# One decoder layer on one core: projections and self-attention in one stage, with the last batch's projections inside the first attention slots

## The reference, cut to what matters

```
y = _layernorm(x, ln1_w, ln1_b)
qkv = (y @ w_qkv).reshape(b, n, 3, H, DK)
attn = softmax(einsum('bhnd,bhmd->bhnm', q, k) / sqrt(DK))
y = einsum('bhnm,bhmd->bhnd', attn, v) ... @ w_proj
x = x + y
```

## Time and profile before

| | us |
|---|---|
| median of 3 runs (lowest, highest) | 1640.35 (1637.45, 1640.81) |
| the profiled execution | 1641.96 |
| its span, first to last instruction | 1640.2 |
| PE busy | 1514.0 (92%) |
| DVE busy | 1118.4 (68%) |
| ACT busy | 870.0 (53%) |
| POOL busy | 378.9 (23%) |
| stage project_qkv, first transpose to last copy of v | 390.6 to 504.6 |
| stage self_attention, first score to last exponential | 513.9 to 1239 |

### The profile page before, as it was taken

How to read it: one execution, slowest core, us unless ns; L and a number is a source line. 1 busy time by engine, 2 the same in 40 slices (tenths; PEclk the granted TensorE clock), 3 DMA queues, 4 the chain that set the end, 5 groups by cost and what they waited for, 6 DMA issues and landing times. The chain is left out here.

```text
span 1640.2 us, 44928 instructions
## 1 busy us (share of the span) xinstructions
PE 1514.0 (92%) x18412; PEld 1078.9 (66%) x18412; DVE 1118.4 (68%) x1679; ACT 870.0 (53%) x1577; POOL 378.9 (23%) x601
## 2 busy tenths in 40 slices
PE   6999699986886999999999999999998939999997
PEld 3555366653542666666666766666666839999997
DVE  4546398886645898889889888988974753333332
ACT  1222465654441788888888888888885301111111
POOL 4110222222431111111111111111110113454453
PEclk9999799999996999999999999999999859999999
DMA  7000000000322111111111111111103935655652
GB/s 227 1 0 20 20 2 2 1 2 20 131 87 103 36 37 39 42 38 37 42 39 37 39 40 38 38 40 38 38 21 105 311 108 195 212 191 198 212 190 81
DMA packets 80330, 125.38 MB, mean 76 GB/s; under 512 B 22243, under 2 KB 46437, under 8 KB 80134
## 3 DMA queue, kind: packets, MB, share of 16 engines
q1 hardware_dynamic: 74518, 107.24, 21.0%
q0 software_dynamic: 5616, 15.34, 2.6%
HBM read 96.03 MB, written 26.08 MB: 74 GB/s over the span
## 5 line engine op out<-in xcount | busy, mean ns | idle before, releaser
L1287 DVE TENSOR_REDUCE sb_m_mx<-banks 128x1 f32<-128x1024 f32 x512 | 603.3, 1220 | 70.6 <-PE banks L1155 62.9
L1253 ACT ACTIVATE sb_m_pT<-banks 128x512 f32<-128x512 f32 x1024 | 556.6, 595 | 117.7 <-PE banks L1182 106.6
L1182 PE MATMUL banks<-sb_m_q,sb_m_k 99*32 99x512 bf16 x4096 | 467.6, 381 | 0.9 <-ACT sb_m_pT L1253 0.5
L1155 PE MATMUL banks<-sb_m_k,sb_m_q 96*32 96x512 bf16 x4096 | 368.0, 388 | 12.9 <-DMA sb_m_k<-k_parts 10.5
L1197 PE MATMUL banks<-sb_m_pT,sb_m_v 128*32 128x256 f32 x4096 | 314.5, 378 | 0.7 <-ACT sb_m_pT L1253 0.7
L1182 PEld LDWEIGHTS banks<-sb_m_q,sb_m_k 99*32 99x32 bf16 x4096 | 179.1, 96 | 79.2 <-ACT sb_m_pT L1253 6.0
L1155 PEld LDWEIGHTS banks<-sb_m_k,sb_m_q 96*32 96x32 bf16 x4096 | 160.3, 96 | 93.0 <-DVE sb_m_mx L1287 20.1
L1197 PEld LDWEIGHTS banks<-sb_m_pT,sb_m_v 128*32 128x32 f32 x4096 | 177.4, 109 | 58.0 <-ACT sb_m_pT L1253 1.2
L1800 ACT ACTIVATE sb_e_hT<-banks 128x512 f32<-128x512 f32 x78 | 46.6, 597 | 237.9 <-PE banks L1760 237.9
L1125 POOL CAST sb_m_mx_parts<-sb_m_mxT 8x128 bf16<-8x128 f32 x64 | 18.1, 283 | 592.4 <-issue 564.4
L1760 PEld LDWEIGHTS banks<-sb_e_xT,w 128*128 128x128 f32 x1248 | 148.1, 195 | 4.3 <-DVE sb_e_xT L1810 2.4
(11 more groups left out here) (216 smaller groups left out, 1876.4 us busy)
## 6 DMA issues: line engine op xcount, KB each, us to landing
w<-in_w SPq DMA_DIRECT2D x47, 1024.0 KB, 5.2
sb_m_q<-q_parts SPq DMA_DIRECT2D x384, 32.0 KB, 1.8
sb_m_k<-k_parts SPq DMA_DIRECT2D x384, 32.0 KB, 1.8
q_parts<-sb_c_parts SPq DMA_DIRECT2D x24, 256.0 KB, 2.2
k_parts<-sb_c_parts SPq DMA_DIRECT2D x24, 256.0 KB, 2.3
X<-in_x SPq DMA_DIRECT2D x4, 1024.0 KB, 10.7
x_rows<-X SPq DMA_DIRECT2D x8, 512.0 KB, 9.5
z_rows<-sb_g_zs SPq DMA_DIRECT2D x8, 512.0 KB, 5.1
```

Of the source, the lines that this page charges most:

```text
L1155: mm = pe.matmul(ps[2 * (k % 2) + h][c:c + 32, :], q_s[0:R, i, k * P + c:k * P + c + 32], k_s[0:R, i, h * 512:(h + 1) * 512], start=True, ...
L1182: mm = pe.matmul(ps[rotating(use)][c:c + 32, :], k_s[:, i2, m * P + c:m * P + c + 32], q_s[:, i2, h * 512:(h + 1) * 512], start=True, stop ...
L1253: act.activation(pT[:, m, h * 512:(h + 1) * 512], ps[rotating(f"b{m}{h}")][:, :], ACT.Exp).then_inc(exped, 1)
L1287: dve.tensor_reduce(mx[:, par % 2, k:k + 1], pz[:, 2 * (k % 2):2 * (k % 2) + 2, :].rearrange("p q n -> p (q n)"), AX.X, ALU.max).then_inc( ...
```

## The change

project_qkv and self_attention give way to one stage, project_and_attend, with one block. The instructions of the attention's slots are those of before, line for line, but for what is shown here. What moves:

- **The last batch.** Batches 0 to 2 are projected ahead as before. The four units of batch 3 stand in slot 0, a half before each "a", and its v in slot 1, a tile before each "a". VectorE's four remainders of batch 3 stand in slot 0 behind the tops 0, 2, 4 and 6. The maxima turned in slot 1 take bank 7, and the last banks of v are 4, 5, 6 and 5.
- **The order in batches 0 to 2.** xT is double (xT_mem and vblk_mem). TensorE transposes the next batch before it makes v of this one; ScalarE copies those tiles out around the last middle. VectorE's order is: both halves and norm of r = 0, first_half of r = 1, remainder 0, second_half, remainder 1, norm, remainder 2, remainder 3. GpSimd makes both powers ahead of the batch's four lows.
- **The fill of rows 96 to 98 of k_s** comes behind remainder 3 of batch 2 on VectorE; TensorE waits for it before slot 0.
- **SyncE** loads head 0 behind the stores of batch 1 and head 1 behind those of batch 2, stores the units of batch 3, and then goes on with slot 1: the load of head 2, the maxima of head 0, and so on.
- **Memory.** xs_c and one xT lie in the upper half of y_all, the other xT and the remainders in vblk_mem and kblk_mem. All loops over batches are written out.

```
 SyncE
+            for b in range(B):
+                for u in range(U):
+                    store(b, u)
+                if b == 1:
+                    batch_stored(0)
+                    load(0, 0)
+                if b == 2:
+                    load(1, 1)
...
-                if has(s, -1, edge):
+                if s > 0 and has(s, -1, edge):
+                    if (s + 1) % H == 0:
+                        batch_stored((s + 1) // H)
 GpSimd
+            for b in range(B):
+                if b < B - 1:
+                    scale(b, 0)
+                    scale(b, 1)
+                for u in range(U):
+                    pool.wait_ge(mid_done, U * b + u + 1)
+                    need(pool, stored[u % 2], 48 * (U // 2 * b + u // 2))
+                    pool.tensor_tensor(parts[:, u % 2, 2, :], rest[:, u % 2, :], parts[:, u % 2, 1, :],
+                                       ALU.subtract).then_inc(low_done, 1)
...
+                    if (s - 2) % H == 0:
+                        pool.wait_ge(v_copied, v_ready((s - 2) // H))
 TensorE
+            turn_tiles(0)
+            for b in range(B - 1):
+                for u in range(U):
+                    unit(b, u, 0)
+                    unit(b, u, 1)
+                turn_tiles(b + 1)
+                for i in range(TPB):
+                    values(b, i)
+
+            pe.wait_ge(set_up, 3)
...
+                if s == 0:
+                    unit(B - 1, 0, 0)
+                    for k in range(TPB):
+                        if k < TPB - 1:
+                            unit(B - 1, (k + 1) // 2, (k + 1) % 2)
+                        a(k)
+                    return
+                if s == 1:
+                    for k in range(TPB):
+                        values(B - 1, k)
+                        a(k)
+                        if k == 2:
+                            maxima()
+                    return
 ScalarE
+            take_tiles(0, 0)
+            take_tiles(0, 1)
+            for b in range(B):
+                for u in range(U):
+                    if u >= 1:
+                        middle(b, u - 1)
+                    high(b, u)
+                if b < B - 1:
+                    take_tiles(b + 1, 0)
+                middle(b, U - 1)
+                if b < B - 1:
+                    take_tiles(b + 1, 1)
+                    for u in range(2):
+                        act.wait_ge(v_done, 2 * b + u + 1)
+                        take_values(b, 4 + 2 * u, 4 * u, 2)
 VectorE
+            for b in range(B - 1):
+                first_half(b, 0)
+                second_half(b, 0)
+                norm(b, 0)
+                first_half(b, 1)
+                remainder(b, 0)
+                second_half(b, 1)
+                remainder(b, 1)
+                norm(b, 1)
+                remainder(b, 2)
+                remainder(b, 3)
+                if b == B - 2:
+                    dve.memset(k_s[R:R + 3, :, :], -1.0).then_inc(set_up, 1)
...
+                for k in range(4):
+                    top(k)
+                    if s == 0 and k in (0, 2):
+                        remainder(B - 1, k // 2)
...
+                for k in range(4, TPB):
+                    top(k)
+                    if s == 0 and k in (4, 6):
+                        remainder(B - 1, k // 2)
 decoder
-                    tensors(ahead, [("w_qkv", [P, KT, 3 * D], F32), ("ln1_w", [P, KT], F32), ("ln1_b", [P, KT], F32),
-                                    ("xs_c", [P, TPB, D], F32)])
+                    tensors(ahead, [("w_qkv", [P, KT, 3 * D], F32), ("ln1_w", [P, KT], F32), ("ln1_b", [P, KT], F32)])
+                    half = t["y_all"][:, B * H // 2:, :, :].rearrange("p h n d -> p (h n d)")
+                    t["xs_c"] = half[:, 0:TPB * D].rearrange("p (n d) -> p n d", d=D)
+                    t["xT_mem"] = half[:, TPB * D:].rearrange("p (k n) -> p k n", k=KT)
                     t["qkv_in"] = ahead.enter_context(nc.semaphore("qkv_in"))
                     run(cross_attention)
-                    run(project_qkv)
-                run(self_attention)
+                    run(project_and_attend)
```

365 lines of the change are left out of this document (added).

## The result

| | before | after |
|---|---|---|
| median, lowest to highest, us | 1640.07 (1637.45 to 1640.81) | 1616.25 (1612.86 to 1618.15) |
| profiled execution, its span | 1641.96, 1640.2 | 1616.15, 1614.2 |
| first transposes of the stage to b(0, 0) | 143.4 | 117.7 |
| b(0, 0) to the start of the last exponential | 704.6 | 703.0 |

What follows compares the result with a forecast made beforehand. TensorE bounds the attention from slot 2, so only the stretch before shrinks: b(0, 0) from 533.94 to 509.5, 24.4 us, or 26.8 at full clock. Taking 25 from 1641.96 gives 1617.0, 1615.4 against the median; range 1608 to 1625.

Steps and rivals of the forecast that it cites:

- The frame: Attention from slot 2 on: bound by TensorE and left alone, so an earlier b(0, 0) is carried to the end.
- Batches 0 to 2: Projection ahead of slot 0: 26.8 us a batch in place of 29.1, remainder 3 of batch 2 ending at 471.2.
- the ring of 29.1: Old batches: transposes wait for the previous batch's v, that for remainder 3, that for the norm; 29.1 us a batch.
- Slot 0: Batch 3's units beside the "a": TensorE 8 x 2.2 = 17.6 us, to 492.4; remainder 3 ends at 495.2.
- Slot 1: Batch 3's v beside the "a": VectorE through at 506.0 after 10.8 us, TensorE a little before.
- SyncE's queue: End of slot 1: head 2's load and the maxima's DMAs stand behind the last store, putting b(0, 0) at 509.5.
- the new wait: TensorE at b(0, 0), for the maxima: some 3.5 us behind the work that was before it.
- The clock: Start of slot 2: half clock cost up to 2.4 us before; gain 26.8 at full clock, 24.4 if it falls again.
- The norm beside two lows: VectorE's norm r = 1 in batches 0 to 2: stretched from 15.8 to 22.1 by GpSimd's lows, at no cost.
- keep 29: Rival, batches 0 to 2: they keep 29.1 us, b(0, 0) comes 7 us later, time 1622; chance 0.12.
- both rivals of the half clock: TensorE at half clock in slots 0 and 1 (1637, or 1630 for slot 0 alone; 0.06), or already in batches (1694; 0.04).
- the slower one: Rival, batches 0 to 2: half clock where TensorE waits for remainders and stores, 45.8 us a batch, 1694; chance 0.04.

Runs made afterwards that it cites:

- e1: Changed kernel with batch 3 projected ahead of slot 0, so slots 0 and 1 hold only scores and maxima; 1623.22 us, ratio 0.9887.
- e9: Changed kernel with the old order on VectorE and GpSimd and one xT, only the one stage left; 1620.66 us.
- e5: Changed kernel with slots 0 and 1 in pairs: a whole unit or two tiles of v, then two "a"; 1615.67 us.
- e3: Changed kernel with head 2's load issued behind the second store of batch 3, not the fourth; 1611.50 us, ratio 0.9818.
- e4: Changed kernel with head 3's load too issued on SyncE before the DMAs of head 0's maxima; 1622.23 us.
- e6: Changed kernel with the fill moved to the head of VectorE's stream, ahead of the first bn_stats; 1620.84 us.
- e7: Changed kernel with GpSimd beginning a batch's lows only when the norm r = 1 is done; 1628.76 us.
- e2: Changed kernel with the old order of VectorE and GpSimd in batches 0 to 2, xT still double; 1629.44 us, ratio 0.9935.
- e8: Changed kernel with one xT, the next batch's transposes behind v again, VectorE's new order kept; 1626.98 us, ratio 0.9916.
- e11: Changed kernel with old order and double xT, plus five unused matmuls on TensorE ahead of each batch's transposes; 1621.06 us.

## Why the prediction was right, and where only its number was

**The frame held.** The steady slots are untouched (11.07 us each in both kernels), so what slot 2 gained stayed. But b(0, 0) at 509.73, where 509.5 was forecast, is partly luck: the stage began 1.5 us later. Counted from the first transposes, 118.9 was forecast and 117.7 measured.

**The number.** The stage gained 27.5 us in the profiles, near the 26.8 that the prediction had for full clock; it took 25. The median fell by 23.8, because 1.5 went to the later start and because the profiled execution of the kernel before lies 1.9 above its median. That 25 and 23.8 agree so well is luck too.

**Where the 25.7 came from.** The profiles of before, e1 and after cut at the start of remainder 3 of batch 2, and e9 beside them:

```profile
473.16 1.23 DVE L1001 SCALAR_TENSOR_TENSOR sb_c_rest<-banks,sb_c_parts 128x1024 f32<-128x1024 f32 x1 [0.19 <-DVE xs_c L988]
...
470.38 1.23 DVE L517 SCALAR_TENSOR_TENSOR kblk_mem<-banks,sb_m_parts 128x1024 f32<-128x1024 f32 x1 [2.03 <-ACT sb_m_parts L421]
...
468.90 1.22 DVE L520 SCALAR_TENSOR_TENSOR kblk_mem<-banks,sb_m_parts 128x1024 f32<-128x1024 f32 x1 [2.04 <-ACT sb_m_parts L424]
...
470.20 1.21 DVE L520 SCALAR_TENSOR_TENSOR kblk_mem<-banks,sb_m_parts 128x1024 f32<-128x1024 f32 x1
```

The first transposes lie at 390.58, 393.53, 392.05 and 393.18 in these profiles. So up to the cut it takes 82.6 before and 76.9 after, 5.7 us; from it to b(0, 0) 60.8 before, 46.9 in e1, 40.8 after. The 13.9 between before and e1 are the joint between the stages, with the meeting of the engines, the fill and the load of head 0, and in them some 2 that e9 gives to the transposes of batch 3 ahead of v: the joint alone is about 12. The last 6.1 are the overlap of batch 3. The prediction gave joint and overlap as one sum, 21; with those 2 they are 20. It had 3 for the batches up to the cut, where 5.7 came.

**"Batches 0 to 2" is the step that failed in its cause.** It forecast 26.8 a batch and it was 26.0, and the chain by which it was worked out is the one in the trace: the norm ends, then a high part that waited 3.9 for its store. But it gave as the reason that the double xT breaks the ring of 29.1. e9 has that ring whole, on the old order, and batches of 27.9, 27.0 and 27.0; at the cut it stands at 77.0, where the kernel before had 82.6. So nearly all of the 5.7 came neither from the double xT nor from the order. The kernel before ran at half clock for 3.4 us in its v of batches 0 and 1. The second half of v of batch 0, before and in e9:

```profile
415.73 5.41 PE L941 MATMUL banks<-w_qkv,sb_c_xT 128*128 128x256 f32 x16 [2.11 <-DVE sb_c_rest L1001]
...
417.48 3.72 PE L274 MATMUL banks<-w_qkv,y_all 128*128 128x256 f32 x16 [1.82 <-DVE kblk_mem L520]
```

That is 1.7 in each of the two batches. Its third batch, at full clock, took 27.7 against 27.0 in e9, and in each batch 0.7 to 0.8 are left. A part of it shows in the rows: before, VectorE idles 0.2 us behind its own bn_stats and norm ([0.19 <-DVE xs_c L988] above), and in e9 it doesn't. Whether that is the loops on the engines was not tried by itself. Nor is it shown that the kernel before always loses the clock there, as there is only one profile of it. The two parts of the change that the step was about bring 2.0 us together.

**Terms that were mis-sized.** "Slot 0" and "Slot 1" counted TensorE's pace as the sum of the matmuls: 2.20 and 1.32 a step, measured 2.46 and 1.61. This is the change from fp32 matmuls to bf16 ones of 32 columns, which e5 halves. Counted from the end of the batches' last remainder, TensorE was to be through slot 1 within 34.8 us and took 37.5, and SyncE's queue stayed about where it was. So the new wait is 1.28 + 0.20 in place of 3.5. "SyncE's queue" is right in place and in the price of an issue: e3 takes the wait away, e4 lengthens it by just the 5.5 us of 12 issues. The fill, which was to cost nothing, costs 0.42 behind batch 2 and 3.6 at the head (e6). "The clock" had up to 2.4 for the start of slot 2 and took 0.6. From b(0, 0) to the first exponential of head 1 are 12.6 us before and 11.4 in e3, which is at full clock and has no wait either, so it is 1.2. The other 0.6 of slot 2's 1.8 are a part of the new wait that slot 2 makes up for. In slots 0 and 1 the half clock cost nothing before, since VectorE set the pace.

**The norm beside two lows.** 6.3 (22.1 less 15.8) was forecast for it and 5.67 measured; it changed nothing, since remainder 2 came behind a high part. e7 shows that it is the lows. The Trainium skill, page "SBUF — State Buffer", section "Who interferes with whom", says that a tensor_scalar of VectorE in a two-port mode and a GpSimd instruction keep each other out for the whole instruction. The traces agree, 2.66 with no low, 4.50 with one, 5.67 with parts of two; which mode the tensor_scalar ran in no trace shows.

**The rivals.** SyncE's queue does hold b(0, 0), by 1.5 us. The batches didn't keep 29, though not for the reason given. TensorE stayed at 1.00 through slots 0 and 1, 20.00 and 11.51 us busy of 20 and 12, so both rivals of the half clock fell. Yet the mechanism of the slower one is real: in e2, e7 and e8 TensorE waits longer in the batches, and the clock from 390 to 475 is 0.92 to 0.94. The 3.4 us that half clock cost the kernel before, and the changed kernel doesn't pay, are a part of its gain that no step of the prediction priced. e4 and e6 show that the changed kernel's clock can fall in batch 0 as well, at no cost there.

## What to carry to other kernels

Before crediting a buffer or an order with a gain, undo each alone and both together: here each alone made the kernel slower by 9 to 13 us, and only the pair paid, by 2. Work that is moved beside other work is worth the difference of the critical chains, not its length: 18 us of a batch's work put into 19 us of slots with room on TensorE gained 6 and another 1 by the clock, while the joint between two stages gave 12. When a stage is pulled into another, look at the shared issue queue next: small DMAs that a late store stands ahead of were the new wait, and moving one load ahead of them was the cheapest further gain.

## What the runs showed of the hardware that was not expected

In e2 TensorE's clock fell to 1.2 GHz in each of its three waits for the norm (5.99, 5.68 and 5.70 us), and the transposes behind them took 3.67 us in place of 1.97. Five matmuls with no use in these waits gave back 6.5 us (e11). The waits in the rows don't tell in advance: the kernel before lost the clock in the second half of v of batches 0 and 1 behind a wait of 2.11 us and kept it in batch 2 behind the same wait, e9 kept it with 1.26 to 1.82, and e4 lost it in batch 0 with the waits of the changed kernel, which kept it.

Changing between fp32 matmuls of 128 columns of weights and bf16 matmuls of 32 and back costs about 0.3 us: two steps take 4.92 us with two such changes and 4.61 with one (e5).

Now and then a single slot takes 11.3 to 12.0 in place of 11.07, mostly one that starts between 1105 and 1120. In e3 this slot has SyncE issue six loads in 4.21 and 3.98 us where 2.62 and 2.74 are the rule, and b(0, 0) of the slot waits 0.8 us for the maxima. Why the issues are slow there stays open.
